# Shared-key attention: the turned maxima and inverse sums move from the score banks to the maxima banks, and from ScalarE and GpSimd to VectorE

## The chip, the cores and the metric

One core of one Trainium2 chip runs the whole program in a single launch. The metric is device time in microseconds; three runs of the kernel before are given, and one more execution was taken by the hardware profiler. PE is TensorE, PEld its weight load, DVE is VectorE, ACT is ScalarE, POOL is GpSimd, SP issues the DMAs.

## The reference, cut to what matters

Eight layers run one after the other on 2048 tokens of width 256, each as `x = layernorm(x + layer(x))`. The change lies in the third, an attention in which 16 query heads of size 16 share one key and one value head:

```
q = (x @ Wq).reshape(Bsz, Tlen, H, D)      # H = 16, D = 16
k = x @ Wk                                 # one key head for all
v = x @ Wv
scores = jnp.einsum('bihd,bjd->bhij', q, k) / jnp.sqrt(jnp.float32(D))
scores = jnp.where(causal, scores, -jnp.inf)
attn = jax.nn.softmax(scores, axis=-1)
out = jnp.einsum('bhij,bjd->bihd', attn, v).reshape(Bsz, Tlen, C)
return out @ Wo + bo
```

The kernel runs it on one sequence of 2048 tokens.

## The kernel before, in words

The 2048 queries are cut into four chunks `c` of 512 columns (CH), and the 16 heads into four groups `g` of G1 = 4. One pair (c, g) is an **item** `i = 4 c + g`, 16 in all. An item has 4 (c + 1) **blocks**: 128 keys by 512 queries, for four heads. `Plan1` lists all 160 blocks and walks through them in **steps** `n`; what each of the five engines does in a step is written out by hand in `l1_pe`, `l1_act`, `l1_dve`, `l1_pool` and `l1_sp`, in that order on each engine, with semaphores between them.

An item goes through these stages.

1. *Maxima* (`unit`). PE multiplies queries by keys with the queries on the partitions, into one of two pairs of PSUM banks (0 and 1, or 2 and 3), and DVE takes the row maximum of the pair (L1351). The pair that a unit takes goes by its number in `unit_ring`: unit x waits until x - 2 is drained. The units of an item are spread over the steps of the item before and are done 7 steps (AHEAD1) before its first block.
2. *Maxima as rows* (`turn_maxima`, `maxima_rows`, `parts`). POOL splits the maxima into three bf16 parts (L1301 to L1304). Four steps before the item's first block PE turns them (L1132), ACT copies the 12 x 512 result out of PSUM (L1245), and SP sends it by DMA (L983) into rows of the queries' tensor, so that the score matmul subtracts the maximum itself.
3. *Scores, exponentials, values*. In each step PE makes four score tiles of block n + 1 (L1146, with a mask matmul L1149 on the diagonal), ACT takes their exponentials (L1257), and PE multiplies those of block n by the values into bank 7 (L1159). Scores take banks 4, 5 and 6 in turn, numbered in `score_ring`; a turn of maxima or of inverse sums takes a number of the same ring.
4. *Division by the sum*. After an item's last block ACT copies the values out (`values_out`, L1263, tile OT). One step later PE gathers the sums of the four heads (`sums`, L1174, in a bank pair of the maxima), DVE takes the inverse (L1363), and POOL spreads it over 32 columns (`spread`, L1310). Three steps after the item's end PE turns it to rows (`turn_inverse`, L1183), ACT copies it to SBUF (`inverse_out`, L1268, tile RD), and POOL multiplies OT by RD into AN (`normed`, L1318).
5. *Output* (`out`, L1196): AN times Wo, for chunks 0 to 2 within the steps of the last item, for chunk 3 behind them, and then the layer norm.

What sets the order around the change is this part of `Plan1.__init__`, with `first[i]` the first block of item i:

```
self.mt_at[self.first[i] - 4] = i
...
self.rdt_at[self.first[i + 1] + 3] = i
```

Chunk 0 has 4 steps for each item, chunk 1 has 8, chunk 2 has 12, chunk 3 has 16. So in the first chunks the turn of one item's inverse (step first[i+1] + 3) stands right ahead of the turn of a later item's maxima (its first block less 4), one step on: items 0 and 3, 1 and 4, 3 and 5, 4 and 6, 5 and 7, 6 and 8. POOL has in this order `parts`, `spread`, `normed` within a step.

Of the kernel before, what the change touches and what calls it, by code (L numbers as in the profile page):

```python
# [14 lines left out]
P = 128  # L15
# [790 lines left out]
class Plan1:  # L806


    def __init__(self):
# [38 lines left out]
        for c in range(NC - 1):  # L848
# [4 lines left out]
            self.turn_at[s + TPC + 4] = c  # L853
        self.unit_ring, self.den_ring, self.score_ring, self.mt_ring, self.rdt_ring = {}, {}, {}, {}, {}
        a = b = 0
        for n in self.steps:
            for u in self.units_at[n]:
                self.unit_ring[u] = a
                a += 1
            if n in self.den_at:  # L860
                self.den_ring[self.den_at[n]] = a
                a += 1
            if n in self.mt_at:
                self.mt_ring[self.mt_at[n]] = b
                b += 1
            if 0 <= n + 1 < self.nb:
                for r in range(G1):
                    self.score_ring[n + 1, r] = b
                    b += 1
            if n in self.rdt_at:  # L870
                self.rdt_ring[self.rdt_at[n]] = b
                b += 1

# [21 lines left out]
def l1_alloc(k):  # L895
# [24 lines left out]
    a.OT = take([P, 2, CH])  # L920
    a.RD = take([P, 2, CH])
    a.w = take([P, KT, QKV1])
# [31 lines left out]
def l1_sp(k, sp, I):  # L954
# [23 lines left out]
    def maxima_rows(i):  # L978
        c, g = i // 4, i % 4
        sp.wait_ge(a.e2, P1.mt_ring[i] + 1)  # L980
        if i >= 1:
            sp.wait_ge(a.mrow, 16 * i)
        sp.dma_start(a.QS[SROWS:SROWS + MROWS, G1 * g:G1 * (g + 1), CH * c:CH * (c + 1)],  # L983
                     a.MT[0:MROWS * G1, i % 2, :]).then_inc(a.mrow, 16)
# [113 lines left out]
def l1_pe(k, pe):  # L1098
# [7 lines left out]
    def unit(u):  # L1106
# [17 lines left out]
        last.then_inc(a.s1, 1)  # L1124

    def turn_maxima(i):
        x = P1.mt_ring[i]
        pe.wait_ge(a.mp, i + 1)
        if x >= 3:
            pe.wait_ge(a.e2, x - 2)  # L1130
        for t in range(TPC):
            last = pe.transpose(PSb[0:MROWS * G1, 4 + x % 3, P * t:P * (t + 1)],  # L1132
                                a.Mp[:, i % 2, t, :, :].rearrange("p a h -> p (a h)"), k.identb[:, :])
        last.then_inc(a.s2, 1)

    def score(n, r):
        i, j, lo = P1.blocks[n]
        c, g = i // 4, i % 4
        x = P1.score_ring[n, r]
        if n == P1.first[i] and r == 0:  # L1140
            pe.wait_ge(a.mrow, 16 * (i + 1))
        if x >= 3:
            pe.wait_ge(a.e2, x - 2)
        b = 4 + x % 3
        rows = SROWS + MROWS
        last = pe.matmul(PS[:, b, lo:CH], a.KS[0:rows, P * j:P * (j + 1)], a.QS[0:rows, G1 * g + r, CH * c + lo:CH * (c + 1)],  # L1146
                         start=True, stop=j < TPC * c)
        if j >= TPC * c:
            last = pe.matmul(PS[:, b, lo:lo + P], k.identb[:, :], a.mkb, start=False, stop=True)  # L1149
        last.then_inc(a.s2, 1)  # L1150

    def value(n):
        i, j, lo = P1.blocks[n]
        c = i // 4
        if j == 0 and i >= 1:
            pe.wait_ge(a.ot, i)
        pe.wait_ge(a.e2, P1.score_ring[n, G1 - 1] + 1)
        for r in range(G1):
# [4 lines left out]
    def sums(i):  # L1163
        x = P1.den_ring[i]
        pe.wait_ge(a.ot, i + 1)
        if i >= NI1 - 2:
            b = T1_BANK + i - (NI1 - 2)
            pe.wait_ge(k.xt_done, 3 * NC - 1)
        else:
            b = 2 * (x % 2)  # L1170
            if x >= 2:
                pe.wait_ge(a.m1, x - 1)
        for t in range(TPC):
# [3 lines left out]
    def turn_inverse(i):  # L1177
        x = P1.rdt_ring[i]
        pe.wait_ge(a.rx, i + 1)
        if x >= 3:  # L1180
            pe.wait_ge(a.e2, x - 2)
        for t in range(TPC):
            last = pe.transpose(PS[:, 4 + x % 3, P * t:P * (t + 1)], a.RX[:, i % 2, t, :, :].rearrange("p r d -> p (r d)"),  # L1183
                                k.ident[:, :])
        last.then_inc(a.s2, 1)

    def out(c, j):
        t = TPC * c + j
        if j == 0:
            pe.wait_ge(a.an, 4 * (c + 1))  # L1190
            pe.wait_ge(k.r_done, NC * 2 + c)
        if t == 0:
            pe.wait_ge(a.ldo, 16 * 4)
            pe.wait_ge(a.m1, P1.unit_ring[P1.last_unit[-1]] + 1)
        for g in range(4):
# [40 lines left out]
def l1_act(k, act, st):  # L1236
    a, PS = k.l1, k.PS
    PSb = PS[:, :, :].bitcast(BF16)

    def maxima_rows(i):  # L1240
        x = P1.mt_ring[i]
        act.wait_ge(a.s2, x + 1)
        if i >= 2:
            act.wait_ge(a.mrow, 16 * (i - 1))
        act.activation(a.MT[0:MROWS * G1, i % 2, :], PSb[0:MROWS * G1, 4 + x % 3, 0:CH], ACT.Copy).then_inc(a.e2, 1)  # L1245

    def exps(n):
# [6 lines left out]
        for r in range(G1):  # L1254
            x = P1.score_ring[n, r]
            act.wait_ge(a.s2, x + 1)
            act.activation(a.PB[:, n % 3, r, lo:CH], PS[:, 4 + x % 3, lo:CH], ACT.Exp, scale=D0 ** -0.5).then_inc(a.e2, 1)  # L1257

    def values_out(i):
        act.wait_ge(a.pv, P1.first[i + 1])  # L1260
        if i >= 2:
            act.wait_ge(a.an, i - 1)
        act.activation(a.OT[:, i % 2, :], PS[:, 7, :], ACT.Copy).then_inc(a.ot, 1)  # L1263

    def inverse_out(i):
        x = P1.rdt_ring[i]
        act.wait_ge(a.s2, x + 1)
        act.activation(a.RD[:, i % 2, :], PS[:, 4 + x % 3, :], ACT.Copy).then_inc(a.e2, 1)  # L1268

    for n in P1.steps:  # L1270
        if n in P1.mt_at:
            maxima_rows(P1.mt_at[n])
        if 0 <= n + 1 < P1.nb:
            exps(n + 1)
        if n + 1 in P1.first[1:]:
            values_out(P1.first.index(n + 1) - 1)
        if n in P1.rdt_at:
            inverse_out(P1.rdt_at[n])
        if n in P1.turn_at:
# [4 lines left out]
def l1_pool(k, pool, st):  # L1284
# [7 lines left out]
    def parts(i):  # L1292
# [4 lines left out]
        if i >= 2:  # L1297
            pool.wait_ge(a.s2, P1.mt_ring[i - 2] + 1)
        nm = a.NM[:, i % 2, :, :]
# [34 lines left out]
def l1_dve(k, dve, st):  # L1334
    a, PS = k.l1, k.PS
    flat = PS[:, :, :].rearrange("p b n -> p (b n)")

# [19 lines left out]
    def inverse(i):  # L1357
# [1392 lines left out]
```

## Time and profile before

| what | value |
|---|---|
| median of 3 runs | 1840.79 us (1836.72 to 1841.16) |
| profiled execution | 1839.08 us, of which the span from first to last instruction is 1837.0 us |
| busy over the span | PE 91%, DVE 54%, ACT 42%, POOL 22% |
| third layer | from 213.6 us to about 777 us of the span |

A busy share is an average over eight layers with different limits, so what follows is read from the third layer alone.

### The profile page before, as it was taken

How to read it: one execution, taken by the hardware profiler on the slowest of the kernel's cores; microseconds unless marked ns; L12 is line 12 of the kernel's file. 1: busy time of each engine (PE TensorE's matmuls, PEld its weight loads, DVE VectorE, ACT ScalarE, POOL GpSimd, SP SyncE). 2: the span in 40 equal slices, each digit the busy share in tenths (PEclk: the TensorE clock that was granted, in tenths of full speed). 3: DMA queues.
4: the chain of work that ended last, by engine and by line, in shares of the span. 5: the costliest groups of instructions: out<-in, count | busy, mean ns of one | idle time of the engine just before them, and what ended most of it. 6: DMA issues, size and time to landing. Idle time of an engine off the chain costs nothing.

```text
span 1837.0 us, 25324 instructions
## 1 busy us (share of the span) xinstructions
PE 1669.1 (91%) x9852; PEld 987.9 (54%) x9852; DVE 996.3 (54%) x1703; ACT 772.9 (42%) x1789; POOL 406.7 (22%) x473
## 2 busy tenths in 40 slices
PE   7999788989999999689997988977999999989998
PEld 4666443434333335445554546754777777764556
DVE  4666665667787771352444853315666676741222
ACT  2422245657767776322111121126566666642110
POOL 2321001011110000220000058504444444540000
PEclk9999688989999999889998999988999999999999
DMA  5000120000000002010000030000000020000000
GB/s 169 3 7 18 52 70 2 1 1 1 2 1 2 1 2 97 0 48 0 0 1 15 1 115 1 0 6 1 7 1 7 1 78 1 1 1 0 12 12 23
DMA packets 28360, 34.96 MB, mean 19 GB/s; under 512 B 5713, under 2 KB 24722, under 8 KB 27730
## 3 DMA queue, kind: packets, MB, share of 16 engines
q1 hardware_dynamic: 28242, 33.35, 5.8%
q8 instruction: 79, 1.29, 0.3%
q14 instruction: 39, 0.32, 0.1%
HBM read 23.74 MB, written 2.10 MB: 14 GB/s over the span
## 4 chain that ended last, share of the span: by engine, by line
PE 71%; DVE 12%; POOL 7%; issue 6%; ACT 3%; DMA 0%; SPq 0%; POOLq 0%; DVEq 0%; ACTq 0%
PE PS L1159 7%; PE PS L1405 6%; PE PS L1146 6%; PE PS L1411 6%; PE PS L1121 6%; PE PS L1426 5%; PE PS L2244 3%; PE PS L2233 2%; PE PS L1907 2%; DVE arena L1351 2%; PE PS L2211 2%; PE PS L1890 2%; PE PS L339 2%; POOL arena L2429 2%; PE PS L2186 2%
## 5 line engine op out<-in xcount | busy, mean ns | idle before, releaser
L1351 DVE TENSOR_REDUCE arena<-PS 128x1 f32<-128x1024 f32 (+7 forms) x320 | 329.9, 1061 | 133.5 <-PE PS L1123 96.0
L1257 ACT ACTIVATE arena<-PS 128x512 f32<-128x512 f32 (+3 forms) x640 | 318.0, 533 | 162.0 <-PE PS L1149 74.8
L1146 PE MATMUL PS<-arena 99*128 99x512 bf16 (+3 forms) x640 | 208.4, 357 | 1.6 <-ACT arena L1257 1.0
L1121 PE MATMUL PS<-arena 96*128 96x512 bf16 (+3 forms) x640 | 182.6, 364 | 14.2 <-DVE arena L1351 13.5
L190 POOL TENSOR_TENSOR rstd<-ve,mhalf 128x4 f32<-128x4 f32 x32 | 32.3, 1010 | 599.7 <-DVE ve L218 599.7
L1159 PE MATMUL PS<-arena 128*32 128x512 f32 (+3 forms) x1280 | 154.8, 556 | 2.8 <-ACT arena L1263 1.7
L185 ACT ACTIVATE XT<-PS 128x1024 f32<-128x1024 f32 x32 | 32.8, 1024 | 273.4 <-PE PS L178 273.4
L1146 PEld LDWEIGHTS PS<-arena 99*128 99x128 bf16 x640 | 61.1, 100 | 153.4 <-ACT arena L1257 112.7
L1405 PE MATMUL PS<-XT,arena 128*128 128x512 f32 x256 | 122.7, 602 | 5.6 <-DVE R L200 3.5
L2244 PE MATMUL PS<-arena 128*128 128x256 f32 x512 | 121.0, 379 | 2.0 <-DVE R L200 2.0
L1411 PE MATMUL PS<-XT,arena 128*128 128x512 f32 x256 | 120.3, 592 | 0.0
L2349 ACT ACTIVATE arena<-PS,arena 128x128 f32<-128x128 f32 x256 | 113.9, 465 | 1.1 <-DVE arena L2525 1.1
L1426 PE MATMUL PS<-arena 128*128 128x256 f32 x512 | 112.2, 379 | 0.9 <-DVE R L200 0.9
L200 DVE TENSOR_TENSOR R<-PS,X 128x1024 f32<-128x1024 f32 x21 | 25.6, 1221 | 156.4 <-PE PS L1426 94.3
L1426 PEld LDWEIGHTS PS<-arena 128*128 128x128 f32 x512 | 96.9, 190 | 17.5 <-issue 2.9
L2244 PEld LDWEIGHTS PS<-arena 128*128 128x128 f32 x512 | 97.0, 190 | 16.2 <-issue 3.2
L2440 POOL TENSOR_TENSOR arena<-arena 128x512 f32<-128x512 f32 x64 | 66.6, 1041 | 127.3 <-DVE arena L2531 127.3
L1121 PEld LDWEIGHTS PS<-arena 96*128 96x128 bf16 x640 | 59.0, 102 | 64.6 <-DVE arena L1351 29.6
L1405 PEld LDWEIGHTS PS<-XT,arena 128*128 128x128 f32 x256 | 48.6, 192 | 67.0 <-issue 60.4
L2521 DVE TENSOR_REDUCE arena<-PS 128x4 f32<-128x512 f32 x64 | 44.0, 687 | 75.0 <-PE PS L2211 75.0
L1411 PEld LDWEIGHTS PS<-XT,arena 128*128 128x128 f32 x256 | 48.8, 191 | 61.8 <-issue 55.8
L178 PE MATMUL PS<-ident,X 128*128 128x128 f32 x256 | 38.6, 301 | 41.3 <-DVE X L227 41.3
(242 smaller groups left out, 2857.7 us busy)
## 6 DMA issues: line engine op xcount, KB each, us to landing
arena<-arena SPq DMA_DIRECT2D x55, 128.0 KB, 2.4
XT<-in_L_attn_xT SPq DMA_DIRECT2D x4, 512.0 KB, 6.7
X<-in_L_attn_x SPq DMA_DIRECT2D x4, 512.0 KB, 9.4
arena<-in_L_attn_out_w SPq DMA_DIRECT2D x1, 2048.0 KB, 7.3
out<-X SPq DMA_DIRECT2D x4, 512.0 KB, 2.9
arena<-in_dmask SPq DMA_DIRECT2D x1, 1024.0 KB, 5.7
arena<-in_L_ffn_W_up SPq DMA_DIRECT2D x1, 1024.0 KB, 5.8
arena<-in_L_ffn_W_gate SPq DMA_DIRECT2D x1, 1024.0 KB, 7.9
```

The costliest lines, as they stand in the source:

```text
L1121: last = pe.matmul(flat[:, o:o + w], q, a.KS[0:SROWS, CH * kc:CH * kc + w], start=True, stop=kc < c)
L1146: last = pe.matmul(PS[:, b, lo:CH], a.KS[0:rows, P * j:P * (j + 1)], a.QS[0:rows, G1 * g + r, CH * c + lo:CH * (c + 1)], start=True, stop= ...
L1159: last = pe.matmul(PS[32 * r:32 * r + 32, 7, lo:CH], a.VX[:, j, :], a.PB[:, n % 3, r, lo:CH], start=j == 0, stop=j == TPC * (c + 1) - 1)
L1257: act.activation(a.PB[:, n % 3, r, lo:CH], PS[:, 4 + x % 3, lo:CH], ACT.Exp, scale=D0 ** -0.5).then_inc(a.e2, 1)
L1351: dve.tensor_reduce(dst, src, AX.X, ALU.max, negate=True).then_inc(a.m1, 1)
L1405: last = pe.matmul(PS[:, n % 2, :], a.gate[:, kt, P * it:P * (it + 1)], k.XT[:, kt, CH * c:CH * (c + 1)], start=kt == 0, stop=kt == KT - 1)
L1411: last = pe.matmul(PS[:, 2 + n % 2, :], a.up[:, kt, P * it:P * (it + 1)], k.XT[:, kt, CH * c:CH * (c + 1)], start=kt == 0, stop=kt == KT - 1)
L1426: last = pe.matmul(f_tile(k, j), a.h[:, c % 2, it, P * j:P * (j + 1)], a.down[:, it, :], start=it == 0, stop=it == HT - 1)
L2244: last = pe.matmul(f_tile(k, t % TPC), a.AT[:, n % 4, i, :], a.W12[:, h, :], start=h == 0, stop=h == H - 1)
L2349: last = act.activation(a.Pr[:, n % 3, i, :], S[:, i, :], ACT.Exp, bias=a.NM[:, t, h:h + 1], scale=a.rq[:, t, h:h + 1], accum_out=a.L[:, t ...
L2440: pool.tensor_tensor(p, p, bc(a.L[:, t, hs], 2, WK3), ALU.mult).then_inc(a.pn, 1)
L2521: st.link(dve.tensor_reduce(a.NM[:, t, hs], S, AX.X, ALU.max))
```

## The change

The maxima's bank pairs become one ring for four kinds of work: units, sums, turned maxima and turned inverses; the three score banks hold scores alone. A turned tile of maxima is copied out by DVE (`maxima_rows` in `l1_dve`), no longer by ACT. A turned tile of inverses isn't copied at all: DVE multiplies OT by it straight from PSUM (`normed` in `l1_dve`), where ACT had copied it and POOL had multiplied. The tile RD and two semaphores' uses go. The last two items' inverses turn into banks 4 and 5. The diff, cut to its core:

```
--- before.py
+++ after.py
@@ -851,25 +851,19 @@
                 self.out_at[s + j] = (c, j)
             self.sum_at[s + TPC] = c
             self.turn_at[s + TPC + 4] = c
-        self.unit_ring, self.den_ring, self.score_ring, self.mt_ring, self.rdt_ring = {}, {}, {}, {}, {}
-        a = b = 0
+        self.unit_ring, self.den_ring, self.mt_ring, self.rdt_ring = {}, {}, {}, {}
+        a = 0
         for n in self.steps:
+            if n in self.mt_at:
+                self.mt_ring[self.mt_at[n]] = a
+                a += 1
             for u in self.units_at[n]:
                 self.unit_ring[u] = a
                 a += 1
-            if n in self.den_at:
-                self.den_ring[self.den_at[n]] = a
-                a += 1
-            if n in self.mt_at:
-                self.mt_ring[self.mt_at[n]] = b
-                b += 1
-            if 0 <= n + 1 < self.nb:
-                for r in range(G1):
-                    self.score_ring[n + 1, r] = b
-                    b += 1
-            if n in self.rdt_at:
-                self.rdt_ring[self.rdt_at[n]] = b
-                b += 1
+            for ring, at in ((self.den_ring, self.den_at), (self.rdt_ring, self.rdt_at)):
+                if n in at:
+                    ring[at[n]] = a
+                    a += 1
 
     def units_by(self, n):
...
@@ -977,7 +970,7 @@
 
     def maxima_rows(i):
         c, g = i // 4, i % 4
-        sp.wait_ge(a.e2, P1.mt_ring[i] + 1)
+        sp.wait_ge(a.m1, P1.mt_ring[i] + 1)
         if i >= 1:
             sp.wait_ge(a.mrow, 16 * i)
...
@@ -1123,20 +1116,23 @@
                 last = pe.matmul(flat[:, o + n - P:o + n], k.identb[:, :], a.mqb, start=False, stop=True)
         last.then_inc(a.s1, 1)
 
+    def free_pair(x):
+        if x >= 2:
+            pe.wait_ge(a.m1, x - 1)
+        return 2 * (x % 2)
+
     def turn_maxima(i):
-        x = P1.mt_ring[i]
+        b = free_pair(P1.mt_ring[i])
         pe.wait_ge(a.mp, i + 1)
-        if x >= 3:
-            pe.wait_ge(a.e2, x - 2)
         for t in range(TPC):
-            last = pe.transpose(PSb[0:MROWS * G1, 4 + x % 3, P * t:P * (t + 1)],
+            last = pe.transpose(PSb[0:MROWS * G1, b, P * t:P * (t + 1)],
                                 a.Mp[:, i % 2, t, :, :].rearrange("p a h -> p (a h)"), k.identb[:, :])
-        last.then_inc(a.s2, 1)
+        last.then_inc(a.s1, 1)
 
     def score(n, r):
         i, j, lo = P1.blocks[n]
         c, g = i // 4, i % 4
-        x = P1.score_ring[n, r]
+        x = G1 * n + r
         if n == P1.first[i] and r == 0:
             pe.wait_ge(a.mrow, 16 * (i + 1))
...
-        pe.wait_ge(a.e2, P1.score_ring[n, G1 - 1] + 1)
+        pe.wait_ge(a.e2, G1 * (n + 1))
         for r in range(G1):
             last = pe.matmul(PS[32 * r:32 * r + 32, 7, lo:CH], a.VX[:, j, :], a.PB[:, n % 3, r, lo:CH],
                              start=j == 0, stop=j == TPC * (c + 1) - 1)
         last.then_inc(a.pv, 1)
 
     def sums(i):
...
-        x = P1.den_ring[i]
         pe.wait_ge(a.ot, i + 1)
         if i >= NI1 - 2:
             b = T1_BANK + i - (NI1 - 2)
             pe.wait_ge(k.xt_done, 3 * NC - 1)
         else:
-            b = 2 * (x % 2)
-            if x >= 2:
-                pe.wait_ge(a.m1, x - 1)
+            b = free_pair(P1.den_ring[i])
         for t in range(TPC):
             last = pe.matmul(PS[:, b, G1 * t:G1 * (t + 1)], a.OT[:, i % 2, P * t:P * (t + 1)], a.denrow, start=True, stop=True)
         last.then_inc(a.s1, 1)
 
     def turn_inverse(i):
-        x = P1.rdt_ring[i]
+        if i >= NI1 - 2:
+            b = 4 + i - (NI1 - 2)
+            pe.wait_ge(a.e2, G1 * P1.nb)
+        else:
+            b = free_pair(P1.rdt_ring[i])
         pe.wait_ge(a.rx, i + 1)
-        if x >= 3:
-            pe.wait_ge(a.e2, x - 2)
         for t in range(TPC):
-            last = pe.transpose(PS[:, 4 + x % 3, P * t:P * (t + 1)], a.RX[:, i % 2, t, :, :].rearrange("p r d -> p (r d)"),
+            last = pe.transpose(PS[:, b, P * t:P * (t + 1)], a.RX[:, i % 2, t, :, :].rearrange("p r d -> p (r d)"),
                                 k.ident[:, :])
-        last.then_inc(a.s2, 1)
+        last.then_inc(a.s1, 1)
 
     def out(c, j):
         t = TPC * c + j
         if j == 0:
-            pe.wait_ge(a.an, 4 * (c + 1))
+            pe.wait_ge(a.m1, P1.rdt_ring[4 * c + 3] + 1)
             pe.wait_ge(k.r_done, NC * 2 + c)
         if t == 0:
             pe.wait_ge(a.ldo, 16 * 4)
-            pe.wait_ge(a.m1, P1.unit_ring[P1.last_unit[-1]] + 1)
...
@@ -1235,14 +1230,6 @@
 
 def l1_act(k, act, st):
     a, PS = k.l1, k.PS
-    PSb = PS[:, :, :].bitcast(BF16)
-
-    def maxima_rows(i):
-        x = P1.mt_ring[i]
-        act.wait_ge(a.s2, x + 1)
-        if i >= 2:
-            act.wait_ge(a.mrow, 16 * (i - 1))
-        act.activation(a.MT[0:MROWS * G1, i % 2, :], PSb[0:MROWS * G1, 4 + x % 3, 0:CH], ACT.Copy).then_inc(a.e2, 1)
 
     def exps(n):
         i, j, lo = P1.blocks[n]
@@ -1252,30 +1239,21 @@
         if n >= 3:
             act.wait_ge(a.pv, n - 2)
         for r in range(G1):
-            x = P1.score_ring[n, r]
+            x = G1 * n + r
             act.wait_ge(a.s2, x + 1)
             act.activation(a.PB[:, n % 3, r, lo:CH], PS[:, 4 + x % 3, lo:CH], ACT.Exp, scale=D0 ** -0.5).then_inc(a.e2, 1)
 
     def values_out(i):
         act.wait_ge(a.pv, P1.first[i + 1])
         if i >= 2:
-            act.wait_ge(a.an, i - 1)
+            act.wait_ge(a.m1, P1.rdt_ring[i - 2] + 1)
         act.activation(a.OT[:, i % 2, :], PS[:, 7, :], ACT.Copy).then_inc(a.ot, 1)
 
-    def inverse_out(i):
-        x = P1.rdt_ring[i]
-        act.wait_ge(a.s2, x + 1)
-        act.activation(a.RD[:, i % 2, :], PS[:, 4 + x % 3, :], ACT.Copy).then_inc(a.e2, 1)
-
     for n in P1.steps:
-        if n in P1.mt_at:
-            maxima_rows(P1.mt_at[n])
         if 0 <= n + 1 < P1.nb:
             exps(n + 1)
         if n + 1 in P1.first[1:]:
             values_out(P1.first.index(n + 1) - 1)
-        if n in P1.rdt_at:
-            inverse_out(P1.rdt_at[n])
         if n in P1.turn_at:
             tail_act(k, act, 3 * NC + P1.turn_at[n], P1.turn_at[n], T1_BANK)
...
@@ -1295,7 +1273,7 @@
         else:
             pool.wait_ge(a.nm, i - 7)
         if i >= 2:
-            pool.wait_ge(a.s2, P1.mt_ring[i - 2] + 1)
+            pool.wait_ge(a.s1, P1.mt_ring[i - 2] + 1)
         nm = a.NM[:, i % 2, :, :]
         part = lambda p: a.Mp[:, i % 2, :, p, :]
         st.link(pool.tensor_copy(part(0), nm))
@@ -1306,24 +1284,14 @@
     def spread(i):
         pool.wait_ge(a.m1, P1.den_ring[i] + 1)
         if i >= 2:
-            pool.wait_ge(a.s2, P1.rdt_ring[i - 2] + 1)
+            pool.wait_ge(a.s1, P1.rdt_ring[i - 2] + 1)
         pool.tensor_copy(a.RX[:, i % 2, :, :, :], bc(a.RT[:, i % 2, :, :], 3, 32)).then_inc(a.rx, 1)
-
-    def normed(i):
-        c, g = i // 4, i % 4
-        pool.wait_ge(a.e2, P1.rdt_ring[i] + 1)
-        if i == 0:
-            for par in range(2):
-                pool.wait_ge(a.stack[par], 16 * SPLIT_DMAS * 2)
-        pool.tensor_tensor(a.AN[:, g, CH * c:CH * (c + 1)], a.OT[:, i % 2, :], a.RD[:, i % 2, :], ALU.mult).then_inc(a.an, 1)
 
     for n in P1.steps:
         if n in P1.mt_at:
             parts(P1.mt_at[n])
         if n in P1.den_at:
             spread(P1.den_at[n])
...
@@ -1362,7 +1331,27 @@
             dve.wait_ge(a.rx, i - 1)
         dve.reciprocal(a.RT[:, i % 2, :, :], PS[:, b, 0:TPC * G1].rearrange("p (t r) -> p t r", t=TPC)).then_inc(a.m1, 1)
 
+    def maxima_rows(i):
+        x = P1.mt_ring[i]
+        dve.wait_ge(a.s1, x + 1)
+        if i >= 2:
+            dve.wait_ge(a.mrow, 16 * (i - 1))
+        dve.tensor_copy(a.MT[0:MROWS * G1, i % 2, :], PSb[0:MROWS * G1, 2 * (x % 2), 0:CH]).then_inc(a.m1, 1)
+
+    def normed(i):
+        c, g = i // 4, i % 4
+        x = P1.rdt_ring[i]
+        b = 2 * (x % 2) if i < NI1 - 2 else 4 + i - (NI1 - 2)
+        dve.wait_ge(a.s1, x + 1)
+        if i == 0:
+            for par in range(2):
+                dve.wait_ge(a.stack[par], 16 * SPLIT_DMAS * 2)
+        dve.wait_ge(a.ot, i + 1)
+        dve.tensor_tensor(a.AN[:, g, CH * c:CH * (c + 1)], a.OT[:, i % 2, :], PS[:, b, :], ALU.mult).then_inc(a.m1, 1)
+
     for n in P1.steps:
+        if n in P1.mt_at:
+            maxima_rows(P1.mt_at[n])
         for u in P1.units_at[n]:
             unit(u)
             if u in P1.last_unit and P1.units[u][0] >= 8:
@@ -1373,6 +1362,8 @@
             l1_keys(k, dve, st, LAST1)
         if n in P1.den_at:
             inverse(P1.den_at[n])
+        if n in P1.rdt_at:
+            normed(P1.rdt_at[n])
         if n in P1.sum_at:
             c = P1.sum_at[n]
             dve.wait_ge(a.biased, c + 1)

```

Three places show how the instructions move. On POOL, from the split of item 2's maxima on (COPY 128x512 is `spread`, TENSOR_TENSOR 128x512 is `normed`, each run of CAST to TENSOR_TENSOR 128x4x4 is one item's `parts`), before:

```order
L1310 COPY arena<-arena 128x512 [waits l1_maxima_bank_drained]
L1318 TENSOR_TENSOR arena<-arena 128x512 [waits l1_odd_parts_stacked,l1_even_parts_stacked,l1_scores_bank_drained]
L1301 CAST arena<-arena 128x4x4 [waits l1_scores,l1_maxima_bank_drained]
L1302 TENSOR_TENSOR arena<-arena 128x16 [waits pool_steps]
L1303 CAST arena<-arena 128x4x4 [waits pool_steps]
L1304 TENSOR_TENSOR arena<-arena 128x4x4 [waits pool_steps]
```

and of the change:

```order
L1288 COPY arena<-arena 128x512 [waits l1_maxima_bank_drained]
L1279 CAST arena<-arena 128x4x4 [waits l1_maxima_scores,l1_maxima_bank_drained]
L1280 TENSOR_TENSOR arena<-arena 128x16 [waits pool_steps]
L1281 CAST arena<-arena 128x4x4 [waits pool_steps]
L1282 TENSOR_TENSOR arena<-arena 128x4x4 [waits pool_steps]
```

The multiplication that stood ahead of the split is gone from POOL, and the split waits for no score bank.

On DVE, at the end of item 3 and the start of chunk 1's second item (TENSOR_REDUCE is a unit's maximum, `x15` says that the row stands 15 times), before:

```order
L1363 RECIPROCAL arena<-PS 128x16 [waits l1_sum_inverse_spread,l1_maxima_scores]
L1351 TENSOR_REDUCE arena<-PS 128x1 [waits l1_maxima_parts,l1_maxima_scores]
L1351 TENSOR_REDUCE arena<-PS 128x1 [waits l1_maxima_scores] x15
L1363 RECIPROCAL arena<-PS 128x16 [waits l1_sum_inverse_spread,l1_maxima_scores]
```

and of the change:

```order
L1332 RECIPROCAL arena<-PS 128x16 [waits l1_sum_inverse_spread,l1_maxima_scores]
L1320 TENSOR_REDUCE arena<-PS 128x1 [waits l1_maxima_parts,l1_maxima_scores]
L1320 TENSOR_REDUCE arena<-PS 128x1 [waits l1_maxima_scores] x3
L1350 TENSOR_TENSOR arena<-arena,PS 128x512 [waits l1_values_evacuated,l1_maxima_scores]
L1339 COPY arena<-PS 12x512 [waits l1_maxima_rows,l1_maxima_scores]
L1320 TENSOR_REDUCE arena<-PS 128x1 [waits l1_maxima_scores] x12
L1332 RECIPROCAL arena<-PS 128x16 [waits l1_sum_inverse_spread,l1_maxima_scores]
```

The multiplication and the copy stand back to back between two units.

On PE, at the turn of item 2's maxima (L1132 before, L1128 now) with the score and the unit behind it, before:

```order
L1132 MATMUL PS<-identb,arena 12x128 [waits l1_scores_bank_drained,l1_maxima_parts]
L1132 MATMUL PS<-identb,arena 12x128 x3
L1146 MATMUL PS<-arena 128x384 [waits l1_scores_bank_drained]
L1149 MATMUL PS<-arena,identb 128x128
L1121 MATMUL PS<-arena 128x384 [waits l1_maxima_bank_drained]
```

and of the change:

```order
L1128 MATMUL PS<-identb,arena 12x128 [waits l1_maxima_parts,l1_maxima_bank_drained]
L1128 MATMUL PS<-identb,arena 12x128 x3
L1142 MATMUL PS<-arena 128x384 [waits l1_scores_bank_drained]
L1145 MATMUL PS<-arena,identb 128x128
L1114 MATMUL PS<-arena 128x384 [waits l1_maxima_bank_drained]
```

PE's order is the same; the turn now waits for a pair that DVE has drained.

## Rows read from the trace of the kernel before

**Rows 1.** Page, part 1: busy us, share of the span, instructions

```profile
PE 1669.1 (91%) x9852; PEld 987.9 (54%) x9852; DVE 996.3 (54%) x1703; ACT 772.9 (42%) x1789; POOL 406.7 (22%) x473
```

**Rows 2.** Windows: stretch, length, busy PE PEld DVE ACT POOL, granted clock, DMA share

```profile
230.00:300.00 70.00, 59.98 (x460) 30.54 (x459) 42.25 (x50) 31.84 (x75) 7.61 (x21) 0.84 0.17 47
300.00:420.00 120.00, 105.49 (x728) 44.80 (x729) 74.83 (x78) 69.92 (x143) 11.90 (x25) 0.91 0.00 1
420.00:580.00 160.00, 156.96 (x1081) 61.53 (x1077) 125.07 (x125) 115.20 (x227) 21.95 (x30) 1.00 0.01 1
```

**Rows 3.** Waits of PE from 230 to 757 us: total us, times, longest

```profile
PE PS L1132 <- POOL arena L1304: 19.5, 6, 3.6
PE PS L1121 <- DVE arena L1351: 5.2, 17, 0.6
```

**Rows 4.** Timeline from 284 us: start, us, engine, line, work [idle before, releaser]

```profile
284.60 0.61 PE L1183 MATMUL PS<-ident,arena 128*128 128x128 f32 x4
...
285.77 0.60 ACT L1268 ACTIVATE arena<-PS 128x512 f32<-128x512 f32 x1
286.45 1.26 POOL L1318 TENSOR_TENSOR arena<-arena 128x512 f32<-128x512 f32 x1 [4.82 <-ACT arena L1268]
287.66 0.20 POOL L1301 CAST arena<-arena 128x16 bf16<-128x16 f32 x1
...
288.77 0.59 PE L1132 MATMUL PS<-identb,arena 128*12 128x128 bf16 x4 [3.57 <-POOL arena L1304]
...
291.01 1.94 PE L1159 MATMUL PS<-arena 128*32 128x512 f32 x8
```

**Rows 5.** Windows: all six gaps, two gaps alone, five us behind the first

```profile
253.00:418.00 165.00, 141.46 (x1000) 62.84 (x998) 100.73 (x107) 88.57 (x186) 17.83 (x38) 0.90 0.01 1
...
263.00:273.50 10.50, 6.93 (x33) 2.73 (x32) 3.48 (x4) 3.63 (x7) 2.05 (x5) 0.67 0.00 1
...
343.60:352.00 8.40, 5.32 (x32) 2.22 (x31) 1.91 (x3) 3.24 (x7) 2.04 (x5) 0.80 0.00 1
...
268.00:273.00 5.00, 5.00 (x21) 1.67 (x20) 2.09 (x2) 1.49 (x4) 0.00 (x0) 0.50 0.01 2
```

**Rows 6.** Groups of DVE by form: busy us, mean ns, idle before

```profile
L2537 DVE COPY arena<-PS 128x512 f32<-128x512 f32 x64 | 43.6, 682 | 21.0 <-PE PS L2233 21.0
...
L1462 DVE TENSOR_TENSOR arena<-arena,PS 128x512 f32<-128x512 f32 x32 | 22.0, 687 | 63.5 <-PE PS L1411 63.5
...
L1080 DVE TENSOR_SCALAR arena<-arena 128x512 bf16<-128x512 bf16 x4 | 1.6, 408 | 0.0
```

**Rows 7.** Groups from 230 to 757 us: what ACT and POOL lose

```profile
L1318 POOL TENSOR_TENSOR arena<-arena 128x512 f32<-128x512 f32 x14 | 17.8, 1271 | 84.1 <-ACT arena L1268 84.1
...
L1245 ACT ACTIVATE arena<-PS 12x512 bf16<-12x512 bf16 x16 | 9.2, 578 | 24.1 <-PE PS L1132 24.1
```

**Rows 8.** Timeline at an inverse's turn (433 us) and at a maxima's (600 us)

```profile
433.79 1.22 DVE L1351 TENSOR_REDUCE arena<-PS 128x1 f32<-128x1024 f32 x1 [0.74 <-PE PS L1121]
...
434.47 0.38 PE L1121 MATMUL PS<-arena 96*128 96x512 bf16 x1
...
600.81 0.82 DVE L1351 TENSOR_REDUCE arena<-PS 128x1 f32<-128x640 f32 x1 [0.76 <-PE PS L1123]
...
601.53 0.59 PE L1121 MATMUL PS<-arena 96*128 96x512 bf16 x2
```

**Rows 9.** Timeline of the layer's end, then the window around it

```profile
757.73 0.77 PE L1183 MATMUL PS<-ident,arena 128*128 128x128 f32 x4 [0.18 <-POOL arena L1310]
...
758.26 2.48 POOL L1318 TENSOR_TENSOR arena<-arena 128x512 f32<-128x512 f32 x2 [0.58 <-ACT arena L1268]
...
760.80 9.21 PE L1196 MATMUL PS<-arena 128*128 128x256 f32 x32 [2.30 <-POOL arena L1318]
...
757.00:766.00 9.00, 6.51 (x23) 4.95 (x24) 0.00 (x1) 1.19 (x2) 3.10 (x3) 0.62 0.00 0
```

**Rows 10.** Timeline of the layer's start

```profile
236.00 0.29 PE L1121 MATMUL PS<-arena 96*128 96x128 bf16 x1 [0.52 <-DVE arena L1351]
```

More of the change, by code:

```diff
@@ L920, in l1_alloc @@
     a.OT = take([P, 2, CH])
-    a.RD = take([P, 2, CH])
     a.w = take([P, KT, QKV1])
@@ L1193, in out @@
             pe.wait_ge(a.ldo, 16 * 4)
-            pe.wait_ge(a.m1, P1.unit_ring[P1.last_unit[-1]] + 1)
+            pe.wait_ge(a.m1, P1.mt_ring[NI1 - 1] + 1)
         for g in range(4):
@@ L1324, in l1_pool @@
             spread(P1.den_at[n])
-        if n in P1.rdt_at:
-            normed(P1.rdt_at[n])
         if n in BIAS1_AT:
@@ L1335, in l1_dve @@
     a, PS = k.l1, k.PS
+    PSb = PS[:, :, :].bitcast(BF16)
     flat = PS[:, :, :].rearrange("p b n -> p (b n)")
```

## The prediction

> **What bounds the kernel now.** I read the page first, then windows over the third layer, then PE's waits there, then the timeline at the longest of them. Over the whole span PE is busy 91% and no other engine more than 54% [rows 1], so an edit pays only where PE waits. The windows show where: in chunk 2 PE is busy 157 of 160 us at the full clock, but from 230 to 420 us it is busy 165.5 of 190 us, and its clock is 0.84 and 0.91 [rows 2]. The table of waits gives that idle time one main owner: PE waits six times, 19.5 us in all, at the turn of the maxima for POOL's split; for DVE's maxima it waits 5.2 us in all [rows 3].
>
> The timeline shows such a wait. PE ends the turn of an inverse at 285.21 (284.60 + 0.61); ACT copies it, 0.60 us; POOL multiplies, 1.26 us; only then POOL begins the split (four small operations from 287.66 on), and PE turns the maxima at 288.77, after 3.57 us without work [rows 4]. The split's input isn't late: the units of an item end three steps before the turn of its maxima. The split stands behind POOL's multiplication, which stands behind ACT's copy, and PE has nothing else in its order. The six pairs of items named with the kernel are the six waits.
>
> Each wait is paid a second time. After the first one PE is busy 5.00 of 5 us at clock 0.50, the lower of its two levels, 1.2 GHz, while DVE works 2.09 us of it: PE alone sets the pace [rows 5]. A mean clock m over a stretch L is 2(1 - m)L at the half level: 6.9 us at the first gap, 3.4 us at the fourth, and 33 us over the 165 us that hold all six [rows 5]. Chunk 2, where PE waits for DVE only briefly, stays at 1.00 [rows 2].
>
> **The change, part by part.** *POOL loses `normed`* (1.27 us an item) and *ACT its two copies* (0.58 and 0.60 us an item) [rows 4, 7]. On the items without a gap nothing waited for these: at nothing, with PE's own work as cover. At the six pairs the chain copy, multiplication, split is off PE's path: up to 19.5 us. With the gaps gone the clock has no reason to fall: half of 33 us, 16.5 us. What is late next is the bank pair, below.
>
> *The layer's end.* Now PE ends its last turn at 758.50, POOL multiplies twice (2.48 us) and PE goes on at 760.80 [rows 9]. DVE would multiply the first tile while PE turns the second, and the second in 0.69 us from 758.56: PE goes on near 759.25, 1.5 us earlier. But the window there has clock 0.62, 6.8 us at the half level [rows 9], and it fell before POOL's wait was over. Work begun earlier in a half-clock stretch that ends at the same time gains half: 0.8 us, up to 1.5 us if the stretch is shorter. Gains together: 19.5 + 16.5 + 0.8 = 36.8 us.
>
> *DVE gains two operations an item.* The multiplication's nearest row is a tensor_tensor of the same size with one operand in PSUM, 687 ns. The copy has none: bf16 from PSUM on 12 partitions. Bounds are 408 ns (bf16 in SBUF) and 682 ns (f32 from PSUM) [rows 6]; I take 682, since it reads PSUM. DVE works 1.37 us more an item, 22 us in all. The Trainium skill, "VectorE: DVE Perf Modes", section on the perf-mode tier table, allows a 16-bit copy from PSUM up to twice the rate, which is near the lower bound; the sum would then be some 2 us better. No row here shows it.
>
> *The ring costs PE waits.* A turn takes a number of the pair ring, so the next unit waits for the unit just before the turn, no longer for the one before that, and the unit after for DVE's copy or multiplication. I price it in three places.
> - A turn alone. At 433 us DVE drains a unit from 433.79 to 435.01; PE began its next unit at 434.47 and would now begin at 435.07: 0.6 us late. At 600 us DVE ends at 601.63 and PE began at 601.53: 0.16 us late [rows 8]. Where two units follow at once, the second waits for DVE's 0.69 us too, some 0.85 us together. PE is the bound there, so the waits count. Fifteen such turns (inverses of items 2 and 7 to 13, maxima of items 2 and 9 to 14) at 0.5 us: 7.5 us, bounds 2 and 13.
> - The six pairs. The turn of the maxima waits for the last unit's drain (0.3 to 0.75 us), the next unit for the multiplication (0.2), one more for the copy (up to 0.45): 0.9 us each, 5.4 us, bounds 3 and 9.
> - The start, and cycles where DVE is near its limit. Before the first blocks PE is paced by DVE (it waits 0.52 us for a drain [rows 10]), so two copies count in full: 1.4 us. From 253 to 418 us DVE is busy 100.7 of 165 us; with 11 us more in some 130 us it is at 86%, most where chunk 1 and 2 begin: 1.5 us by my choice, bounds 0 and 5.
>
> Sum of costs: 7.5 + 5.4 + 1.4 + 1.5 = 15.8 us. Net gain 21 us. Against the profiled execution's own 1839.1 us that is 1818.1 us; the runs' median lies 1.7 us above that execution, so about 1819.5 us. No DMA is added; the maxima's rows leave for SBUF 0.1 us later than by ACT's 0.58 us and have three steps to land.
>
> **The rivals.**
> - *The gap closes and the clock doesn't come back.* Short waits of PE for DVE would take the place of the long ones. For it: more such waits than now, up to 1.4 us at a pair. Against it: with 17 waits of up to 0.6 us for DVE [rows 3] the clock in chunk 2 is 1.00 [rows 2]. Gain 21 - 16.5: 1836 us. This is also what the Trainium skill says, "TensorE: Matmul & The Clock Gate", section on the second failure mode, psum-queue depth-cycling: brief idle times between groups that cycle through banks make the clock go up and down. Rows 2 speak against it at today's waits, not yet at tomorrow's. Chance 0.09.
> - *The ring costs double.* Every turn stalls DVE's pipeline by both drain and copy, near the upper bounds (13 + 9 + 1.4 + 5 = 28 us): 1832 us. Chance 0.14.
> - *The ring costs almost nothing*, since DVE runs ahead of the turns and ACT's shorter queue frees score banks sooner: costs 4 us, 1808 us. Chance 0.12.
> - *Slower: DVE becomes the bound.* If each of the 27 turns behind the start (15 alone, 12 in pairs) held PE for a whole drain and DVE's operation, 1.22 + 0.69 = 1.9 us, that is 51 us, and less the 36.8 us gained the kernel takes 1855 us. It decides from 1.36 us a turn on. For it: DVE is at 78% in chunk 2 (125 of 160 us [rows 2]). Against it: PE has 1 us of other work between most units. Chance 0.04.
> - *The change doesn't do what it says*: PE still waits at the six places, for another thing than POOL's multiplication. The split's other input is three steps old, so I see none; it would be 1841 us plus the ring's costs where not hidden, 1850 us. Chance 0.02.
>
> **How the numbers follow.** The forecast, chance 0.59, is 1819.5 us, alone from 1812 to 1827. The measurement can't tell less than 0.3% from no change, that is 5.5 us, so faster means below 1835.3 us. Range: 1806 to 1833 us; it takes in cheap and dear ring costs, and leaves out the clock's rival and the two slow cases (0.15) with a tail. Faster: 0.59 + 0.12 + 0.13 of the dear ring + 0.04 of the clock's rival = 0.88. Slower: 0.06. Same: the rest, 0.06.
>
> **What would show it.** In the profile after: no wait of PE for POOL at the turn of the maxima, where six made 19.5 us; the granted clock 0.98 or more from 253 us to the end of chunk 1; the last block 30 us earlier or less. PE's waits for DVE should grow from 5.2 to about 20 us, the part worked out above. DVE's copy should read 0.4 to 0.7 us and its multiplication 0.69 us; the stretch between the last turn and the output's first matmul should be 0.75 us. The prediction is wrong if PE's waits for DVE in chunks 2 and 3 exceed 15 us, if the clock still falls in chunks 0 and 1, or if something other than POOL held the turns.

## The result, and the profile after

The changed kernel takes 1815.36 us in the median of 4 runs (1813.9 to 1816.45) against 1840.21 us before (4 runs): a ratio of 0.987, with a 95% interval of 0.985 to 0.989. The profiled execution has a span of 1813.3 us where it was 1837.0. The forecast was 1819.5 us, with a range of 1806 to 1833.

The page's first part (busy us, share of the span, instructions) shows what moved: ScalarE has 32 instructions fewer, GpSimd 16 fewer and VectorE 32 more, so only the 16 copies of the inverses are gone altogether. It answers to [rows 1]:

```profile
PE 1660.7 (92%) x9852; PEld 985.2 (54%) x9852; DVE 1010.2 (56%) x1735; ACT 760.0 (42%) x1757; POOL 386.1 (21%) x457
```

The windows of the layer (stretch, length, busy PE PEld DVE ACT POOL, granted clock) answer to [rows 2, 5]:

```profile
230.00:300.00 70.00, 65.76 (x524) 33.58 (x523) 53.27 (x65) 35.53 (x80) 5.06 (x19) 0.91 0.17 47
300.00:380.00 80.00, 77.41 (x576) 33.19 (x579) 63.22 (x71) 51.43 (x105) 5.57 (x20) 1.00 0.01 2
...
253.00:388.00 135.00, 128.89 (x999) 58.53 (x998) 106.87 (x120) 81.81 (x172) 8.96 (x31) 1.00 0.01 2
```

From 253 us on, PE is at the full clock, 2.4 GHz, through chunks 0 and 1, where the mean was 0.90. PE's waits from 230 to 735 us (total, times, longest) answer to [rows 3]:

```profile
PE PS L1114 <- DVE arena L1320: 9.2, 27, 0.6
PE PS L1128 <- DVE arena L1320: 1.7, 6, 0.6
...
PE PS L1178 <- POOL arena L1288: 0.5, 2, 0.3
PE PS L1178 <- DVE arena L1320: 0.4, 1, 0.4
```

The turn of the maxima (now L1128) waits for DVE alone, 1.7 us in six times where it had waited 19.5 us in six for POOL. These aren't the same six: one is the turn of item 0's maxima, ahead of all pairs (0.35 us), four pairs have 0.2 us each, the last pair has 0.60 us, and the pair of items 5 and 7 has none. So 1.4 us stand at the pairs. Waits for DVE's maxima in the units grew from 5.2 to 9.2 us.

The timeline at the last pair, items 6 and 8 (start, us, engine, line; the idle time before and what ended it in brackets), shows the new order of events:

```profile
381.66 1.23 DVE L1320 TENSOR_REDUCE arena<-PS 128x1 f32<-128x1024 f32 x1 [1.25 <-PE PS L1114]
...
381.74 0.60 PE L1178 MATMUL PS<-ident,arena 128*128 128x128 f32 x4
382.80 0.68 DVE L1350 TENSOR_TENSOR arena<-arena,PS 128x512 f32<-128x512 f32 x1
382.94 0.39 PE L1128 MATMUL PS<-identb,arena 128*12 128x128 bf16 x4 [0.60 <-DVE arena L1320]
...
383.39 0.41 DVE L1339 COPY arena<-PS 12x512 bf16<-12x512 bf16 x1
...
383.53 0.61 PE L1114 MATMUL PS<-arena 96*128 96x512 bf16 x2
```

PE turns the inverse, stands 0.60 us until DVE has drained the unit before it, turns the maxima, and goes on to the next unit 0.59 us after that turn began. It had stood 3.08 us at this place.

To see where time goes, four landmarks serve: POOL's spread of an item's inverse sums (L1310 before, L1288 after), whose rows are, for items 0, 7, 13 and 15, before

```profile
256.95 0.61 POOL L1310 COPY arena<-arena 128x512 f32<-128x512 f32 x1 [9.01 <-DVE arena L1363]
428.50 0.61 POOL L1310 COPY arena<-arena 128x512 f32<-128x512 f32 x1 [18.49 <-DVE arena L1363]
663.24 0.61 POOL L1310 COPY arena<-arena 128x512 f32<-128x512 f32 x1 [20.05 <-DVE arena L1363]
757.06 0.62 POOL L1310 COPY arena<-arena 128x512 f32<-128x512 f32 x1 [0.23 <-DVE arena L1363]
```

and after

```profile
259.10 0.61 POOL L1288 COPY arena<-arena 128x512 f32<-128x512 f32 x1 [9.05 <-DVE arena L1332]
399.93 0.61 POOL L1288 COPY arena<-arena 128x512 f32<-128x512 f32 x1 [21.69 <-DVE arena L1332]
640.01 0.61 POOL L1288 COPY arena<-arena 128x512 f32<-128x512 f32 x1 [20.21 <-DVE arena L1332]
734.00 0.61 POOL L1288 COPY arena<-arena 128x512 f32<-128x512 f32 x1 [0.23 <-DVE arena L1332]
```

From item 0 to item 7, which holds all six pairs, 171.55 us became 140.83: 30.7 us gained. From item 7 to 13 (chunks 2 and 3), 234.74 became 240.08: 5.3 us lost. The table holds the same differences for every kernel below; "start" is from ScalarE's last middle part (`l1_middle`, L1054 before) to item 0, "end" from item 15 to the residual sum of chunk 3 (L200), and the last column is the ratio with its interval, each against runs of the kernel before on the same chip.

| kernel | start | 0 to 7 | 7 to 13 | 13 to 15 | end | median us | ratio |
|---|---|---|---|---|---|---|---|
| before | 34.2 | 171.6 | 234.7 | 93.8 | 13.1 | 1840.2 | |
| the change | 35.8 | 140.8 | 240.1 | 94.0 | 12.2 | 1815.4 | 0.987 (0.985 to 0.989) |
| split first | 34.7 | 139.3 | 234.7 | 93.8 | 14.4 | 1806.0 | 0.982 (0.980 to 0.985) |
| inverse part | 35.0 | 140.2 | 238.1 | 94.3 | 11.8 | 1806.7 | 0.984 (0.982 to 0.986) |
| maxima part | 35.6 | 171.0 | 236.7 | 93.5 | 13.1 | 1841.9 | 1.002 (1.000 to 1.004) |
| filled gap | 34.2 | 157.2 | 234.7 | 93.8 | 13.4 | 1828.2 | 0.995 (0.993 to 0.997) |
| first and end | 34.2 | 137.7 | 234.7 | 93.8 | 12.3 | 1803.2 | 0.981 (0.979 to 0.983) |
| delay back | 36.0 | 175.1 | 240.1 | 94.0 | 12.2 | 1847.7 | 1.005 (1.003 to 1.007) |
| copy twice | 35.0 | 141.5 | 240.5 | 94.0 | 10.9 | 1816.9 | 0.987 (0.985 to 0.989) |

The time at which the layer starts differs by up to 10 us from one profile to another (the last middle part begins at 216.84 us with the inverse part and at 226.68 with first and end), although all layers ahead of it are the same code. So pieces within the layer tell small effects better than the whole time, whose 4 to 13 runs of one kernel spread over 2.5 to 14 us. The last three rows of the table ran on another chip than the four above them, so their medians go with their own ratios and not side by side with the others.

The first and the last piece aren't clean either, since the mean granted clock within them differs. The end has 0.72 or 0.73 in the change, the inverse part, first and end, and delay back (11.8 to 12.3 us), and 0.74 in the kernel before, the maxima part and the filled gap (13.1 to 13.4 us); in split first it is 0.64 (14.4 us) and in copy twice 0.84 (10.9 us).

### The profile page after: what moved, and what is told of

It reads as the page before. It is cut to its first block, busy times and chain, and to the rows that moved or that the text cites. A ratio compares the mean times of both kernels' runs of the same rounds, so it can differ in the third digit from the quotient of the medians.

```text
span 1813.3 us, 25325 instructions
## 1 busy us (share of the span) xinstructions
PE 1660.7 (92%) x9852; PEld 985.2 (54%) x9852; DVE 1010.2 (56%) x1735; ACT 760.0 (42%) x1757; POOL 386.1 (21%) x457
## 4 chain that ended last, share of the span: by engine, by line
PE 74%; DVE 13%; POOL 6%; issue 3%; ACT 3%; DMA 0%; SPq 0%; POOLq 0%; DVEq 0%; ACTq 0%
PE PS L1155 7%; PE PS L1142 6%; PE PS L1114 6%; PE PS L1396 6%; PE PS L1402 6%; PE PS L1417 5%; PE PS L2235 3%; DVE arena L1320 3%; PE PS L2224 2%; PE PS L1898 2%; PE PS L2202 2%; PE PS L1881 2%; PE PS L339 2%; POOL arena L2420 2%; PE PS L2177 2%
## 5 line engine op out<-in xcount | busy, mean ns | idle before, releaser
L1114 PE MATMUL PS<-arena 96*128 96x512 bf16 (+3 forms) x640 | 178.4, 357 | 18.3 <-DVE arena L1320 17.5
L190 POOL TENSOR_TENSOR rstd<-ve,mhalf 128x4 f32<-128x4 f32 x32 | 32.3, 1009 | 606.3 <-DVE ve L218 606.3
L1155 PE MATMUL PS<-arena 128*32 128x512 f32 (+3 forms) x1280 | 150.0, 541 | 2.8 <-ACT arena L1250 1.7
L200 DVE TENSOR_TENSOR R<-PS,X 128x1024 f32<-128x1024 f32 x21 | 25.6, 1221 | 148.1 <-PE PS L1417 94.3
```

The lines of the kernel that those rows point to most:

```text
L1114: last = pe.matmul(flat[:, o:o + w], q, a.KS[0:SROWS, CH * kc:CH * kc + w], start=True, stop=kc < c)
L1155: last = pe.matmul(PS[32 * r:32 * r + 32, 7, lo:CH], a.VX[:, j, :], a.PB[:, n % 3, r, lo:CH], start=j == 0, stop=j == TPC * (c + 1) - 1)
```

## The experiments

**Split first.** One edit to the kernel before; the ring, the banks and the engines stay.

```
     for n in P1.steps:
-        if n in P1.mt_at:
-            parts(P1.mt_at[n])
+        if n + 1 in P1.mt_at:
+            parts(P1.mt_at[n + 1])
         if n in P1.den_at:
             spread(P1.den_at[n])
         if n in P1.rdt_at:
             normed(P1.rdt_at[n])
```

> The kernel before with one edit: on GpSimd the split of the maxima stands ahead of the multiplication, one step earlier; no bank, ring or engine is changed. Queue theory (the gain is the wait of PE behind GpSimd's multiplication, 19.5 us, and the clock lost behind it, 17 us, less what the pair ring costs): all of the first and none of the last, 1840 - 36 = 1804 us, no wait of PE for L1304, clock 1.00 from 253 us on. Bank theory (the gain came from score banks that hold scores alone and from a shorter ScalarE queue): no gain, 1840 us.

Measured 1805.98 us. PE's waits hold no row for the turn of the maxima any more. The timeline at items 1 and 4, the pair of [rows 4]:

```profile
274.75 0.22 POOL L1304 TENSOR_TENSOR arena<-arena 128x16 bf16<-128x16 f32 x1
...
278.49 0.60 PE L1183 MATMUL PS<-ident,arena 128*128 128x128 f32 x4
...
279.02 0.39 PE L1132 MATMUL PS<-identb,arena 128*12 128x128 bf16 x4
279.66 0.60 ACT L1268 ACTIVATE arena<-PS 128x512 f32<-128x512 f32 x1
...
280.31 0.34 PE L1146 MATMUL PS<-arena 99*128 99x384 bf16 x1 [0.20 <-ACT arena L1268]
...
280.34 1.28 POOL L1318 TENSOR_TENSOR arena<-arena 128x512 f32<-128x512 f32 x1 [5.36 <-ACT arena L1268]
```

The split is done 4 us before PE wants it; ACT's copy and POOL's multiplication still run; PE waits 0.2 us for that copy at the second score behind the turn, and PE waits for the multiplication nowhere in the middle of the layer. The piece from item 0 to 7 gains 32.3 us, and the pieces from 7 to 15 lose nothing. The start is 0.5 us longer, and the end 1.3 us, at the lower clock given above. The gain is more than the change's 30.7 us, with two lines. The bank theory is out.

**Inverse part.** The changed kernel with the maxima's half of it undone: PE turns maxima into the score ring, and ACT copies them. The edit is shown against the changed kernel, cut.

```
 def turn_maxima(i):
-        b = free_pair(P1.mt_ring[i])
+        x = P1.mt_ring[i]
         pe.wait_ge(a.mp, i + 1)
+        if x >= 3:
+            pe.wait_ge(a.e2, x - 2)
...
 def l1_dve(k, dve, st):
...
-        if n in P1.mt_at:
-            maxima_rows(P1.mt_at[n])
```

> The change's half on the inverse sums alone: turned into the pair ring, VectorE multiplies from PSUM; the maxima's turn stays in the score ring with ScalarE's copy. Queue theory: the wait is gone as in the full change, and about half the ring's cost is spared, 1840 - 37 + 8 = 1811 us. Bank theory: half the gain, about 1828 us.

Measured 1806.68 us. It has the whole gain from item 0 to 7 (31.4 us) and loses 3.4 us from item 7 to 13, where it turns six inverses into the pair ring: 0.57 us each.

**Maxima part.** The other half: maxima in the pair ring with DVE's copy, inverses as before. The edit is again against the changed kernel, cut.

```
 def l1_pool(k, pool, st):
...
+        if n in P1.rdt_at:
+            normed(P1.rdt_at[n])
...
 def l1_dve(k, dve, st):
...
-        if n in P1.rdt_at:
-            normed(P1.rdt_at[n])
```

> The change's half on the maxima alone: turned into the pair ring, VectorE copies; the inverse stays in the score ring with ScalarE's copy and GpSimd's multiplication. Queue theory: the six waits stay, and the ring's cost comes on top, 1840 + 5 = 1845 us, with 18 to 20 us of waits for L1304's successor. Bank theory: half the gain, about 1828 us.

Measured 1841.93 us, a ratio of 1.002: the half by itself isn't told from no change. The table of PE's waits keeps the old wait:

```profile
PE PS L1135 <- POOL arena L1294: 20.0, 6, 3.7
PE PS L1121 <- DVE arena L1342: 5.8, 17, 0.6
```

From item 7 to 13 it loses 2.0 us over six turns of maxima, 0.33 us each. The two halves' losses there add up to 5.3 us, which is what the change lost.

**Filled gap.** The kernel before, with PE kept busy in the six waits; what the added matmuls write is overwritten.

```
         x = P1.mt_ring[i]
-        pe.wait_ge(a.mp, i + 1)
         if x >= 3:
             pe.wait_ge(a.e2, x - 2)
+        if 3 <= i <= 8:
+            for _ in range(12):
+                pe.matmul(PS[:, 4 + x % 3, :], a.KS[0:SROWS, 0:P], a.KS[0:SROWS, 0:CH], start=True, stop=True)
+        pe.wait_ge(a.mp, i + 1)
```

> The kernel before with 12 matmuls of 512 columns, whose result is overwritten, ahead of the wait for GpSimd's split at the maxima of items 3 to 8: the waits' place in time stays, but PE isn't idle in them. If the idle time is what the clock falls for, the half-clock time (34 us) goes and the time is 1840 - 17 = 1823 us, with the split ending no earlier; if the clock falls for another reason, 1840 us or somewhat more.

Measured 1828.23 us. The timeline of the same pair, and the window over all six waits:

```profile
285.52 0.61 PE L1186 MATMUL PS<-ident,arena 128*128 128x128 f32 x4
...
285.96 2.76 PE L1132 MATMUL PS<-arena 96*128 96x512 bf16 x12
...
289.68 0.39 PE L1135 MATMUL PS<-identb,arena 128*12 128x128 bf16 x4 [0.97 <-POOL arena L1307]
```

```profile
253.00:418.00 165.00, 156.96 (x1173) 71.91 (x1171) 110.99 (x118) 99.11 (x209) 17.80 (x39) 1.00 0.01 4
```

The turn of the maxima comes as late as before, 4.2 us behind the turn of the inverse, and POOL's chain is unchanged. But PE has 1.0 us without work in place of 3.6 (3.9 us in all six where it had 19.5), and the granted clock is 1.00 where it was 0.90. The piece from item 0 to 7 is 14.3 us shorter. So the clock's fall hangs on PE's idle time, and of what closing the gaps brings it is 14 us; the forecast of this run had 17.

A second reading gives the same price. These windows run from item 0 to 7 in the kernel before and in the first-and-end kernel below, with the same 1034 matmuls:

```profile
256.95:428.50 171.55, 148.06 (x1034) 64.91 (x1034) 105.89 (x112) 94.33 (x197) 17.83 (x38) 0.90 0.01 1
260.86:398.59 137.73, 133.64 (x1034) 60.88 (x1034) 105.77 (x112) 92.31 (x197) 17.86 (x38) 1.00 0.01 2
```

PE is busy 14.4 us less at the full clock.

**First and end.** The split-first kernel, and for the last two items DVE multiplies from PSUM, out of the score ring; ACT's copy and POOL's multiplication of these two go:

```
+        if n in P1.rdt_at and P1.rdt_at[n] >= NI1 - 2:
+            i = P1.rdt_at[n]
+            x = P1.rdt_ring[i]
+            dve.wait_ge(a.s2, x + 1)
...
+            dve.tensor_tensor(a.AN[:, i % 4, CH * 3:CH * 4], a.OT[:, i % 2, :], PS[:, 4 + x % 3, :], ALU.mult).then_inc(a.an, 1)
```

> The split-first kernel with one more edit: for items 14 and 15 alone VectorE multiplies straight from PSUM (bank of the score ring), no copy by ScalarE and no GpSimd. Queue theory: the middle of the layer as in the split-first run, and 0.8 us less at the end as in the change; 1838.9 - 33 - 1 = 1805 us, PE's wait before L1196 0.8 us where it was 2.3. If the end's half-clock stretch ends at the same time whatever PE does, that 0.8 us is all; if it ends with PE's earlier start, 1.5 us.

Measured 1803.22 us, the lowest median here. From item 0 to 7 it gains 33.8 us with the same code as the split-first kernel: that one's granted clock from 253 to 418 us was 0.99 in its profile, here it is 1.00. PE's wait before the output (L1196) is 0.8 us where it was 2.3, as expected. The end is 0.8 us shorter than before, the lower of the two values expected; against the split-first kernel the medians differ by 2.8 us, on two chips, and less than the runs of either spread, so the whole time doesn't tell the two apart.

**Delay back.** The changed kernel, with a multiplication nobody reads on POOL, behind DVE's:

```
+    def dead(i):
+        pool.wait_ge(a.m1, P1.rdt_ring[i] + 1)
...
+        st.link(pool.tensor_tensor(a.RD[:, 0, :], a.RD[:, 1, :], a.RD[:, 1, :], ALU.mult))
...
         if n in P1.den_at:
             spread(P1.den_at[n])
+        if n in P1.rdt_at and P1.rdt_at[n] < NI1 - 2:
+            dead(P1.rdt_at[n])
```

> The changed kernel with GpSimd's multiplication put back as dead work (its result is read by nobody) behind VectorE's own, ahead of the split, for items 0 to 13. Nothing of banks or engines' real work is changed back. Queue theory: PE waits again at six turns, about 3 us each (VectorE 0.68 + GpSimd 1.27 + split 0.85 and hops), the clock falls again, and all that the change gained in chunks 0 and 1 goes, 1815 + 31 = 1846 us. Bank theory: GpSimd has room, 1815 us.

Measured 1847.74 us. The table of waits and the timeline of the pair of items 1 and 4:

```profile
PE PS L1129 <- POOL arena L1283: 20.1, 6, 4.1
```

```profile
288.99 0.60 PE L1179 MATMUL PS<-ident,arena 128*128 128x128 f32 x4
289.65 0.68 DVE L1361 TENSOR_TENSOR arena<-arena,PS 128x512 f32<-128x512 f32 x1
290.41 1.04 POOL L1297 TENSOR_TENSOR arena<-arena 128x512 f32<-128x512 f32 x1 [5.93 <-DVE arena L1361]
291.52 0.20 POOL L1280 CAST arena<-arena 128x16 bf16<-128x16 f32 x1
...
292.72 0.38 PE L1129 MATMUL PS<-identb,arena 128*12 128x128 bf16 x4 [3.12 <-POOL arena L1283]
```

The six waits are back, the clock from 253 to 418 us is 0.89, and the piece from item 0 to 7 is 34.3 us longer than in the change, with every bank and engine of the change's real work in place. What the change gained came from the place of the split in POOL's order.

**Copy twice.** The changed kernel with DVE's copy of the turned maxima made twice.

```
+        st.link(dve.tensor_copy(a.MT[0:MROWS * G1, i % 2, :], PSb[0:MROWS * G1, 2 * (x % 2), 0:CH]))
         dve.tensor_copy(a.MT[0:MROWS * G1, i % 2, :], PSb[0:MROWS * G1, 2 * (x % 2), 0:CH]).then_inc(a.m1, 1)
```

> The changed kernel with VectorE's copy of the turned maxima made twice (0.41 us and a semaphore more, 16 times, 7 us of VectorE). If the ring's cost is PE waiting one drain at a turn, only the start and the second unit behind a turn see it: 2 us more, 1817 us. If VectorE's added time as such is the cost (it is the bound in chunks 0 and 1), 7 us more, 1822 us.

Measured 1816.93 us. The pieces from item 0 to 7 and from 7 to 13 are 0.7 and 0.4 us longer, together 1.1 us, for the 12 of the 16 added copies that fall into them, 4.9 us of DVE (0.405 us each). DVE's time as such is not what the ring costs.

## Why the prediction was right, point by point

- *What bounds the layer and where the six waits come from*: as forecast. The split-first run shows the place in POOL's order as the cause, the delayed one the reverse.
- *The sum*: 21 us net was forecast, 23.7 us measured on the span (24.9 on the medians); the layer's pieces add up to 24.5. The gains were set 2.1 us too high and the costs 5.6 us too high, so part of the closeness is luck: two errors of opposite sign. (1818.1 and 1.7 make 1819.8 and not 1819.5 us, which changes nothing.)
- *Gap and clock, 19.5 + 16.5 us*: without any cost of the ring, the first-and-end kernel gains 33.8 us from item 0 to 7, so the two terms were 2.2 us too high together. The filled gap puts 14.3 us of it on the clock and so leaves 19.5 for the waits. So the waits were right and the clock was priced some 2 us too high: I took half of all time at the half level, 16.5 us, while PE's busy time differs by 14.4 us. Probably the rest is time at the half level in which PE had no work; that isn't shown.
- *The pairs, 5.4 us, and near-limit cycles, 1.5 us*: too dear. From item 0 to 7 the change takes 3.1 us more than first-and-end, at the same clock of 1.00, while I had 6.9 us plus 1 us for item 2's two turns. (The 1.6 us against split first is no fair measure, since that profile had the clock at 0.99 there.) At the pairs I added three waits. The first kind, the turn's own, made 1.4 us in five of the six places, where I had 0.3 to 0.75 us in each. The other two, at the units behind the turns, don't show: PE's waits in the units are 2.7 us in this piece where they were 2.6. This is the mis-sized term: 4.8 us, which outweighs the gains' excess and makes the forecast too late.
- *A turn alone, 0.5 us*: in chunks 2 and 3 twelve turns cost 5.3 us, 0.44 each; 0.57 for an inverse and 0.33 for maxima. The waits in the units from item 7 to 13 were, before and after:

```profile
PE PS L1121 <- DVE arena L1351: 1.6, 4, 0.6
PE PS L1114 <- DVE arena L1320: 5.2, 13, 0.6
```

  So 3.6 us of the 5.3 are waits for DVE, as the mechanism has it. A further 1.8 us stands in the profile as longer busy time of the same 1584 matmuls (231.3 to 233.1 us); no run explains it.
- *Start 1.4 us, end 0.8 us*: 1.6 lost and 0.9 gained. The start's match isn't shown to come from the two copies counting in full: with the copies doubled the start was 35.0 us, shorter than the change's 35.8, and the granted clock over the piece was 0.76 before and with the copies doubled, and 0.73 in the change. In the change's end window the clock was 0.62 again (733 to 742 us), so the end's half-clock stretch was as long as in [rows 9]. From the last turn's end to the output's first matmul the change has 0.77 us, where 0.75 had been forecast.
- *DVE's copy, 682 ns taken*: 405 ns measured, the multiplication 678 ns, in the groups of DVE from 230 to 735 us (busy us, mean ns, idle before):

```profile
L1350 DVE TENSOR_TENSOR arena<-arena,PS 128x512 f32<-128x512 f32 x15 | 10.2, 678 | 1.0 <-PE PS L1178 1.0
...
L1339 DVE COPY arena<-PS 12x512 bf16<-12x512 bf16 x16 | 6.5, 405 | 4.7 <-PE PS L1128 4.7
```

  The lower bound, 408 ns, was the right end. In the copy-twice run 4.9 us of added copies cost 1.1 us, so the 277 ns too many in each copy are worth less than a microsecond, by my estimate. The Trainium skill, "VectorE: DVE Perf Modes", section on the perf-mode tier table, allows a 16-bit copy from PSUM up to twice the rate. The trace agrees: 405 ns stand against the 682 ns of the f32 copy from PSUM in [rows 6].

- *Waits for DVE of about 20 us*: 11.3 us (9.2 + 1.7 + 0.4), for the reason given at the pairs. From item 7 to 13, in chunks 2 and 3, they are 5.2 us, far from the 15 us named as a sign of being wrong.
- *The clock's rival*: out. With 27 waits of up to 0.6 us the granted clock was 1.00 from 253 us on. The Trainium skill's psum-queue depth-cycling ("TensorE: Matmul & The Clock Gate", section on the second failure mode) did not set in at idle times of this length; it isn't shown where it would.

The bound from below in the rivals, a ring that costs almost nothing, was half true: 10.2 us of ring costs (1.6 + 3.1 + 5.3, and 0.2 from item 13 to 15), with the start's 1.6 us not shown to be the ring's, where 4 and 15.8 had been named.

## What to carry to other kernels

Before moving work between engines or banks, look at what stands ahead of the late instruction on its own engine: here 1 us of work with inputs long ready stood behind another item's chain, and moving it ahead by two changed lines gave 33 us, more than the rebuild that also removed the chain. When PE is the bound, price a gap twice, once as time (19.5 us here) and once as the clock behind it (14 us). And a shared ring of two buffers has a price for each small job put between large ones: here 0.33 us for a turn with a copy of 0.41 us behind it and 0.57 us for one with a multiplication of 0.68 us. Doubling the copy added less than 0.1 us to a turn in the same chunks, so most of the price isn't the small job's own length.

## What the runs showed of the hardware that I had not expected

Useless matmuls can pay: 72 of them (12 at each of six waits, 2.76 us of PE each time) made the kernel 0.5% faster (0.993 to 0.997), by keeping the granted clock at 1.00 over a stretch where it had been 0.90. The start of the layer moved by up to 10 us between profiles of kernels that are the same up to there; the windows from 100 to 216 us show granted clocks between 0.77 and 1.00 in different order, so where the clock falls in the first layers differs from one execution to the next.
